# Three-pass products, a remainder tile and shifted sums in the mixer of a macaron block

## What is computed

```python
z_, xBC, dt_raw = split(rmsnorm(ln(x)) @ in_proj_w.T)       # 256 | 256+32 | 4 columns
y = conv_b + sum(xp[:, k:k+l, :] * conv_w[:, k] for k in range(4))
u, B, C = split(silu(y))
B, C = B / (norm(B) + EPS), C / (norm(C) + EPS)
dt = softplus(dt_raw + dt_bias);  A = exp(A_log)
# over the tokens of a sequence: S = 1/(1 + dt^2 A)
# w = S*(w - dt*A*ys + dt*B*u);  ys = ys + dt*w;  o = ys . C
out = ((o + D*u) * silu(z_)) @ out_proj_w.T
h = x + out;  hn = rmsnorm(h)
return h + (silu(hn @ gate_w.T) * (hn @ up_w.T)) @ down_w.T  # 352 hidden
```

## Time and profile before

| what | value |
|---|---|
| median of 3 runs | 763.55 us (761.63 to 764.13) |
| the profiled execution | 763.67 us, its span 761.9 us |
| PE busy | 639.3 us (84%) |
| DVE busy | 552.5 us (73%) |
| POOL busy | 520.2 us (68%) |
| ACT busy | 373.3 us (49%) |

### The profile page before, as it was taken

How to read it: one execution, slowest core, us unless ns; L and a number is a source line. 1 busy time by engine, 2 the same in 40 slices (tenths; PEclk the granted TensorE clock), 3 DMA queues, 4 the chain that set the end, 5 groups by cost and what they waited for, 6 DMA issues and landing times.

```text
span 761.9 us, 13660 instructions
## 1 busy us (share of the span) xinstructions
PE 639.3 (84%) x3768; PEld 471.6 (62%) x3768; DVE 552.5 (73%) x1706; ACT 373.3 (49%) x705; POOL 520.2 (68%) x656
## 2 busy tenths in 40 slices
PE   3379879999952678999999999898988989999991
PEld 2245458989841246656666666565755658898961
DVE  4665756565628979897989899999875556666638
ACT  1122214545423889675867766564222215454535
POOL 3787784666664886895979768876786735666650
PEclk9998989999985779989999999999999999999997
DMA  9511222333216000000000000000001133333228
GB/s 263 175 44 50 81 70 76 86 92 85 80 35 211 0 1 1 0 2 1 1 1 1 2 8 9 17 12 22 23 29 33 53 98 80 86 89 91 73 64 288
DMA packets 49368, 46.34 MB, mean 61 GB/s; under 512 B 8456, under 2 KB 42861, under 8 KB 49296
## 3 DMA queue, kind: packets, MB, share of 16 engines
q1 hardware_dynamic: 40592, 28.54, 13.4%
q0 software_dynamic: 8704, 16.93, 6.8%
HBM read 25.30 MB, written 21.19 MB: 61 GB/s over the span
## 4 chain that ended last, share of the span: by engine, by line
PE 34%; POOL 29%; issue 15%; DVE 14%; ACT 4%; DMA 2%; SPq 0%; POOLq 0%; DVEq 0%; ACTq 0%
POOL xs L717 13%; POOL ys L733 8%; PE ps_tr L1709 4%; PE ps_tr L2111 3%; PE ps_go L2098 2%; PE ps_go L1709 2%; PE ps_go L1880 2%; PE ps_go L1884 2%; POOL arena L551 1%; PE ps_go L2111 1%; PE ps_a L2085 1%; PE ps_a L2087 1%; PE ps_a L2086 1%; PE ps_b L2085 1%; PE ps_b L2086 1%
## 5 line engine op out<-in xcount | busy, mean ns | idle before, releaser
L733 POOL DMA_INDIRECT ys<-arena,dest x144 | 140.8, 978 | 89.2 <-issue 64.8
L717 POOL DMA_INDIRECT xs<-rows,pos x128 | 127.6, 997 | 50.9 <-issue 36.4
L2111 PE MATMUL ps_tr<-w_down_e,arena 128*128 x384 | 50.7, 275 | 0.0
L1556 DVE TENSOR_TENSOR hid<-silu_a,ps_b 128x512 f32<-128x512 f32 x36 | 24.7, 687 | 35.1 <-ACT silu_a L1048 35.1
L1556 DVE TENSOR_TENSOR hid<-silu_a,ps_a 128x512 f32<-128x512 f32 x36 | 24.7, 687 | 34.5 <-ACT silu_a L1048 34.5
L1028 ACT ACTIVATE silu_a<-ps_a 128x512 f32<-128x512 f32 x32 | 19.1, 597 | 58.0 <-PE ps_a L2049 56.9
L2111 PEld LDWEIGHTS ps_tr<-w_down_e,arena 128*128 128x128 f32 x384 | 46.7, 192 | 0.0
L1523 DVE TENSOR_TENSOR hid<-silu_a,ps_b 128x512 f32<-128x512 f32 x32 | 21.9, 686 | 30.1 <-PE ps_b L2051 28.2
L1057 ACT ACTIVATE arena<-ps_go 128x512 f32<-128x512 f32 x72 | 42.6, 592 | 2.0 <-PE ps_go L2098 2.0
L2098 PE MATMUL ps_go<-ident,hid 128*128 128x128 f32 x288 | 43.2, 272 | 0.2
L2098 PEld LDWEIGHTS ps_go<-ident,hid 128*128 128x128 f32 x288 | 35.6, 140 | 10.0 <-DVE hid L1556 0.5
(11 more groups left out here) (362 smaller groups left out, 1975.8 us busy)
## 6 DMA issues: line engine op xcount, KB each, us to landing
arena<-xs SPq DMA_DIRECT2D x144, 65.0 KB, 1.9
rows<-ys SPq DMA_DIRECT2D x8, 512.0 KB, 3.6
arena<-ys SPq DMA_DIRECT2D x8, 512.0 KB, 7.3
ys<-arena,dest POOLq DMA_INDIRECT x144
x<-in_L_attn_x SPq DMA_DIRECT2D x8, 256.0 KB, 4.8
arena<-in_L_ffn_ew SPq DMA_DIRECT2D x4, 512.0 KB, 7.0
xs<-rows,pos POOLq DMA_INDIRECT x128, 2.3
out<-x SPq DMA_DIRECT2D x8, 256.0 KB, 3.4
```

The lines of the kernel that those rows point to most:

```text
L717: pool.indirect_dma_start(xs, bass.IndirectOffsetOnAxis(pos[:, n, i:i + 1], 0), rows[:, n * TT + i % TT, :], None).then_inc(scattered, 16)
L733: pool.indirect_dma_start(ys, bass.IndirectOffsetOnAxis(dest[:, i:i + 1], 0), y_out[:, p % YRING, j, :], None, bounds_check=2 * TOK - 1, o ...
L1556: dve.tensor_tensor(hid[:, p % 2, 0, :].rearrange("p (j h) -> p j h", j=2), silu_a[:, p % 2, :].rearrange("p (j h) -> p j h", j=2), ps_pai ...
L2111: r = pe.matmul(ps_answers(p)[:, j * P:(j + 1) * P], hid_t[:, p % 2, at:at + P], w_down_e[:, bass.ds(which[2 * p + j], 1), k, :].rearrange ...
```

## The change

Products: the weights of the 17 products are split once into fp32r parts, `hi` (ACT's copy) and `lo` (DVE's difference), and z^T and hn^T likewise: ACT writes z^T rounded to fp32r, DVE subtracts it from the PSUM bank into `zt_lo`. A product is then three passes: hi by z^T, lo by z^T, hi by the remainder. B and C stay fp32 and are done twice, with z^T and with the remainder. hn^T and its remainder lie in `xt_hi` and `xt_lo`.

```diff
+            def zt_low(b, q):
+                n = SQ * b + q
+                dve.wait_ge(zt_ready, 2 * n + 2)
+                step(dve.tensor_copy(zt_lo[:, 0:TAPS - 1], halo_zero[:, :] if q == 0 else zt_lo[:, BT:].bitcast(F32)))
+                dve.scalar_tensor_tensor(zt_lo[:, TAPS - 1:], pb["zt"], col[:, C_NORM1:C_NORM1 + 1], zt[:, TAPS - 1:].bitcast(F32),
+                                         ALU.mult, ALU.subtract).then_inc(zt_lo_ready, 1)
+            def hnt_low(b, q):
+                n = SQ * b + q
+                dve.wait_ge(hnt_ready, n + 1)
+                dve.scalar_tensor_tensor(hnt_lo, pb["hnt"], col[:, C_NORM2:C_NORM2 + 1], hnt.bitcast(F32),
+                                         ALU.mult, ALU.subtract).then_inc(hnt_lo_ready, 1)
...
+            def hi_parts(target, hi, lo, shift, start):
+                pe.matmul(target, hi, zt[:, shift:shift + BT], start=start, stop=False)
+                pe.matmul(target, lo, zt[:, shift:shift + BT], start=False, stop=False)
+            def lo_part(target, hi, shift, stop):
+                return pe.matmul(target, hi, zt_lo[:, shift:shift + BT], start=False, stop=stop)
...
+                pe.wait_ge(hnt_lo_ready, n + 1)
+                for target, at, done in ((pb["gate"][c], c * P, gate_ps_ready), (pb["up"][c], FF + c * P, up_ps_ready)):
+                    pe.matmul(target[0:m], gu_hi[:, at:at + m], hnt, start=True, stop=False)
+                    pe.matmul(target[0:m], gu_lo[:, at:at + m], hnt, start=False, stop=False)
+                    pe.matmul(target[0:m], gu_hi[:, at:at + m], hnt_lo, start=False, stop=True).then_inc(done, 1)
```

```diff
-                step(dve.tensor_tensor(chunks(t5), chunks(t5), spread(flat(cmid)), ALU.subtract))
-                dve.tensor_tensor(t0[q], t5, t3[q], ALU.subtract).then_inc(logs_ready, 1)
+                dve.tensor_tensor(chunks(t5), chunks(t5), spread(flat(cmid)), ALU.subtract).then_inc(logs_ready, 1)
...
-                step(dve.tensor_tensor(t3[q], t3[q], t2[q], ALU.subtract))
...
+                dve.tensor_copy(chunks(t7)[:, :, 0], phase_b[:, :])
+                step(dve.tensor_tensor(chunks(t7)[:, :, 1:], chunks(t3[q])[:, :, 0:CH - 1],
+                                       phase_b[:, :].rearrange("p (c a) -> p c a", a=1).broadcast_to([P, CB, CH - 1]), ALU.add))
...
+                act.activation(bc_tm[:, :, :], tokens, ACT.Copy)
+                act.activation(bc_sq[:, :, :], tokens, ACT.Square).then_inc(bc_sq_ready, 1)
...
+                for t in range(TT):
+                    r = act.activation(hn[:, t, :], hb[:, t, :], ACT.Square, accum_out=hsq[:, t:t + 1])
```

POOL: norms becomes five instructions with one power of 8 columns instead of two of 4:

```diff
+                pool.tensor_scalar(asmall[:, 0, :], var, 1.0 + RMS_EPS, LN_EPS * RMS_EPS, ALU.mult, ALU.add)
+                pool.tensor_scalar(asmall[:, 1, :], var, LN_EPS, None, ALU.add)
+                step(pool.tensor_scalar(asmall[:, 2, :], amv[:, m, :, 0], -1.0, None, ALU.mult))
+                step(pool.tensor_tensor(ascale[:, m, :, :], asmall[:, 0:2, :], minus_half[:, 0:2, :], ALU.pow))
+                pool.tensor_tensor(offset[:, m, :, :], asmall[:, 2:3, :].broadcast_to([P, 2, TT]), ascale[:, m, :, :],
+                                   ALU.mult).then_inc(arstd_ready, 1)
...
-    nc = bacc.Bacc("TRN2", target_bir_lowering=False, num_devices=1)
+    nc = bacc.Bacc("TRN2", target_bir_lowering=False, num_devices=1, dynamic_dma_scratch_size=8192)
```

More of the change, by code:

```diff
@@ L222, in macaron @@
         halo_zero = sb("halo_zero", [P, TAPS - 1])
-        zt = part(1, [P, TAPS - 1 + BT])
+        zt = sb("zt", [P, TAPS - 1 + BT], F32R)
+        zt_lo = sb("zt_lo", [P, TAPS - 1 + BT], F32R)
         zn = part(1, [P, TT, P])
@@ L265, in macaron @@
         refs = sb("refs", [P, TT, CT])
-        turns = sb("turns", [P, 3, CB])
-        phase_c = sb("phase_c", [P, CB])
+        turns = sb("turns", [P, 2, CB])
         phase_b = sb("phase_b", [P, CB])
@@ L395, in early, with first, not_first @@
             return block if block and SQ * block[0] + block[1] < EARLY else None
+        def first(block):
+            return block if block and SQ * block[0] + block[1] == 0 else None
+        def not_first(block):
+            return block if block and SQ * block[0] + block[1] > 0 else None
         def not_last(block):
@@ L1214, in phase_sums @@
                                             ALU.mult, ALU.add))
-                step(dve.tensor_copy(turns[:, 0, :], chunks(t3[q])[:, :, CH - 1]))
-                step(dve.tensor_scalar(turns[:, 1, :], turns[:, 0, :], ROUND, -ROUND, ALU.add, ALU.add))
-                step(dve.tensor_tensor(turns[:, 2, :], turns[:, 0, :], turns[:, 1, :], ALU.subtract))
-                start = 0.0
+                ends = chunks(t3[q])[:, :, CH - 1]
+                step(dve.tensor_scalar(turns[:, 0, :], ends, ROUND, -ROUND, ALU.add, ALU.add))
+                step(dve.tensor_tensor(turns[:, 1, :], ends, turns[:, 0, :], ALU.subtract))
+                start = phase[:, 0, 0:1]
                 if q == 1:
@@ L1390, in body @@
                 do(combined_block, at(4))
+                do(zt_low, first(at(1)))
                 do(state_update, at(-4), 0)
+                do(zt_low, not_first(at(-2)))
                 do(phase_sums, at(-3))
@@ L1404, in body @@
                 do(outputs, at(-4), 1)
+                do(hnt_low, at(-5))
                 do(log_sums, at(-2))
@@ L1704, in transposes @@
                 return r
-            def projected(target, weights, taps):
-                for k in range(taps):
-                    shift = k if taps > 1 else TAPS - 1
-                    r = pe.matmul(target, weights(k), zt[:, shift:shift + BT], start=(k == 0), stop=(k == taps - 1))
-                return r
+            def hi_parts(target, hi, lo, shift, start):
[3 more added lines that the diff above has]
+                return pe.matmul(target, hi, zt_lo[:, shift:shift + BT], start=False, stop=stop)
             def z_features(b, q):
@@ L2264, in laid_out @@
     col[:, C_OFFC] = np.where(part == 0, 0.0, 0.25)
-    col[:, C_OFFB] = np.where(part == 0, 0.25, 0.5)
     arrays["columns"] = col
```

235 lines of the change are left out of this document (133 added, 102 removed).

## The result

The changed kernel takes 777.20 us (median of 4 runs, 773.29 to 781.28), against 763.62 (761.63 to 764.13): ratio 1.0194, 95% interval 1.0169 to 1.0219. It is slower by 13.6 us, where 759.5 was forecast, outside the range. Two repetitions gave 1.0195 (1.0124 to 1.0265) and 1.0229 (1.0176 to 1.0283). The profiled execution is the fastest of the four: 773.29 us, span 771.6, so the trace holds 9.7 us of the loss.

The account below looks back on a forecast made before the run. A ring through PE and ACT, with DVE on it, bounds the kernel. Terms −2.3 (start), −1.6, −0.9 (steady), +1.9 and +0.2 (routing), −1.6 (last), +0.3 (tail) sum to −4.0: forecast 759.5 us, range 749.5 to 767.0.

Parts of the forecast that it names:

- Products and ACT: Mixer: three fp32r passes replace each fp32 product, −2.36 us PE net per block; ACT's part goes from 5.85 to 6.2.
- the stretch: PE from gate start to the end of the last z product: goes from 17.2 to 14.6 us.
- PE's wait: At gate_up of the first chunk in a steady turn: new 1.6 us wait for DVE's remainder of hn^T.
- Steady turns: Mixer turns without routing: 35.7 us against 36.2, from 14.9 (DVE), 14.6 (PE) and 6.2 (ACT); −0.45 each.
- The first turn with routing: Mixer turn where DVE has more work: 39.4 us against 37.5, so +1.9.
- I take 14.9: From zt_copy's end to hnt_low's end on DVE: 14.9 us, with L1188's 1.23 us gone and no wait inherited.
- rival B: Between zt_low and hnt_low, POOL's sums block DVE through the port: 1.1 to 1.5 us per turn, about 767; chance 0.20.
- the turn to the last phases: Second turn with routing, DVE the bound throughout: gains and losses come out even, +0.2 us.
- all of it shifts one to one: End: POOL works without a gap from its gated output, then last routing; earlier gains carry through, tail adds 0.3 us.
- rival E: Halved descriptor scratch makes POOL's scatters wait for room: each 0.2 us adds 5, giving 764.5; chance 0.05.
- norms: Start, POOL on the chain for some three blocks: 5.06 us becomes 2.75, −2.3 each, much of it given back.
- The dt product of the fourth block: End of the start phase: 2.3 us earlier than before, between 0 and 6.9.

Follow-up runs that it names:

- e4: Changed kernel with two POOL sums cut short (h_add to 8 of 128 columns, dt sum to 32 of 512): ratio 1.0086.
- e15: Changed kernel with z^T's remainder behind phase_sums and gate/up's four hn^T passes ahead of the wait for the remainder: 765.56 us, ratio 1.0051.
- e18: e15 with a descriptor scratch of 10240 bytes instead of 8192: ratio 0.9997.
- e10: Changed kernel without DVE's two remainders, the third pass taking z^T or hn^T again: ratio 0.9873, on a slower chip.
- e1: Kernel before the change with only the descriptor scratch cut to 8192 bytes: 767.08 us, ratio 1.0066.
- e6: Changed kernel with one fp32 product for each three passes and no remainders, small scratch kept: ratio 1.0042.
- e14: Changed kernel with gate and up's four passes by hn^T ahead of PE's wait for the remainder: 769.62 us, ratio 1.0111.
- e7: e6 with the full scratch of 16384 bytes: ratio 0.9962.
- e5: Changed kernel with full scratch; low weight parts left out, the second pass taking the high part again: ratio 1.0163.
- e16: e7 run again, unchanged: 762.74 us, ratio 0.9985.
- e17: e7 with three passes for gate and up alone, hn^T's remainder behind outputs 1, and PE's wait split: 759.06 us, ratio 0.9965.
- e9: Changed kernel, unchanged, run again on a chip where every kernel took 8% longer: ratio 1.0195.
- e11: Same two order changes as e15 to the changed kernel, on the slower chip: ratio 0.9971.

## Why the prediction was wrong

**Products and ACT were right, and that PE would wait for DVE's remainder.** The passes are 0.23 us apart, the stretch takes 14.7 us against 14.6, ACT 6.4 against 6.2, z^T's remainder 0.9 against 1.0. That PE's wait is 1.4 us against 1.6 is luck: the remainder came 1.0 us later behind zt_copy than forecast (15.9 against 14.9), and PE itself was ready at 14.5 instead of 13.3, since it had already stood for DVE twice in that stretch (0.50 us for the outputs, 0.27 for the state). Steady turns came out at 37.0 and 36.9 instead of 35.7. The first turn with routing met its forecast (39.7 against 39.4) with 3.4 us at half clock that the forecast did not have, so that in part is luck too.

**The first failed step** is the one that took 1.23 us for L1188 out of DVE's path ("I take 14.9"; measured 15.9). The wait for POOL's sum passed to L1300, and a second sum met L1301: 1.97 us together over their lengths in e4 (1.72 + 1.38 − 0.70 − 0.43), partly paid by a scan that became shorter (1.21 instead of 1.68). That is rival B in place and mechanism, though L1301 has only one tile as input: 36.8 was its steady turn, 36.9 to 37.0 the measured one. B's total of 767 us falls short all the same, since it had none of what follows. It had 0.20 and should have led, since the row stood in the trace and nothing in the change moved POOL's sums off DVE's stretch.

**The second** is that every turn was reckoned at full clock. The forecast knew of the clock only in the start (0.77). The granted clock of the turns from 431 falls to 0.96, 0.84, 0.96 and 0.95, and at 0.4 us for 1 us the 20.5 us more at half clock in 320 to 620 are some 8 us, of which the waits hide a part; the 3.0 us in the turn to the last phases (forecast 0.2) lie in the 0.84. In after each of the five stretches between 320 and 620 begins in a wait of PE of 1.4 us or more, or within 1.5 us behind it (the longest 1.4 us behind the 2.37 us at 481.56, a wait for DVE's gram_copy). But after's waits of 1.93 us at 357.59 and of 1.50 at 394.62 bring none on. e15 and e18 have a stretch of 10 us in turns whose only longer wait is the 1.5 us for zt_copy, and e10's steady turns, with that wait too, have none. Nor does it take a remainder: e1 and e6, which have none, hold 17.0 and 23.9 us at half clock. What brings the stretches on stays open.

**The third** is the end. The forecast took it that POOL has work without a gap from its gated output on and that "all of it shifts one to one". POOL's piece did shift so (30.8 us instead of 30.5), but after, the last routing starts 2.6 us behind POOL's end, at the end of another chain:

```profile
575.85 0.47 PE L2010 MATMUL ps_a<-xt_hi,gu_hi 128*128 128x512 f32 x1 [2.35 <-DVE xt_lo L1291]
```

The last block's gate, 566.3 before, waits for a remainder that DVE makes only behind ffn_add of the block ahead, which waits for PE. The stretch from the last dt product to the first of the last scatters takes 117.9 us before, 125.2 after, 122.0 in e14 and 119.2 in e10, so the remainders are most of it.

**The fourth** is rival E. It had the scratch right as a cost, but as a small lengthening of each scatter, at 0.05. It is four standings (2.69, 1.97, 2.48 and 1.95 us in after), 0.5 to 0.8% in all (e1, e6 against e7, e15 against e18), and should have been a term of the sum.

**Start.** norms came to 3.67 us instead of 2.75, since its power took 2.13:

```profile
278.68 0.51 POOL L545 TENSOR_SCALAR asmall<-amv 128x4 f32<-128x4 f32 x1
...
279.87 2.13 POOL L548 TENSOR_TENSOR ascale<-asmall,minus_half 128x8 f32<-128x8 f32 x1
...
282.35 1.28 POOL L650 TENSOR_TENSOR hid<-hid,silu_a 128x512 f32<-128x512 f32 x1
```

That did not decide the start; the scratch did. The mixer's first dt product stands at 240.0 to 241.3 in the four traces with the new norms and the full scratch (e5, e7, e16, e17), and at 243.1 to 246.5 in the ten with 8192 bytes (without those on the slow chip of e9 to e11); before it is at 243.0. The dt product of the fourth block, forecast 2.3 us earlier than before, is 3.7 earlier in e5 and 0.2 in after. (In e1, with the norms of before, the first dt product is only 0.6 us later than in before.)

Summed: the scratch costs 4 to 6 us, and the three passes with DVE's remainders, whatever part of it goes through the clock, 15 (e5 against e7), less the 1 to 3 us that the rest gives (e16, e7). That makes 16 to 20 us where the three chips gave 13.6 to 17.5; parts taken from different chips don't add up more closely. How the 15 us divide between waits and clock is not shown.

**The chances.** By the chances of its own rivals the forecast's "faster" comes to 0.64 or more and its "slower" to 0.18, where it wrote 0.62 and 0.16. No rival joined the port, the clock, the end and the scratch, which all came at once.

## What to carry to other kernels

When the instruction that a port wait is booked on goes, leave the wait in the sum until the other engine's work has moved, and look for the instruction that inherits it. Work taken off PE pays only if nothing new stands in its ring: put the passes that need no remainder ahead of the wait for it (here 1.2%), and the remainder where its engine would stand anyway (0.6% more). And a setting in a constructor's argument list is part of a change: it cost here more than the rest gained.

## What the runs showed that was not expected

- With 8192 bytes of descriptor scratch POOL stands four times in 272 indirect DMAs (2.66, 1.96, 2.48 and 1.94 us in e1); with 10240 and 16384 bytes it does not (e18, e7). The first standing goes up to 4.02 us (e14), and on the slow chip the one at the 193rd is 7.97 us long (e9).
- A kernel with four needless passes per turn was no slower than the same without, and perhaps faster (1.0174 against 1.0229, with overlapping intervals), with a higher mean clock (0.930 against 0.926).
- Kernels that differ in the scratch alone differ in their half clock: 6.8 us before and 17.0 in e1, 10.3 in e7 and 23.9 in e6 (320 to 620 us, one execution each).
- Executions of after spread over 8 us (773.3 to 781.3), those of before over 2.5, and they go by the clock: 0.928 to 0.912.
